# Value products, spread maxima and an earlier first score in the first attention layer

## The reference

```python
qkv = x @ w_qkv.T + b_qkv                 # 512 q, 128 k, 128 v features
q, k, v = jnp.split(qkv, [q_dim, q_dim + kv_dim], axis=-1)
q = apply_rope(q, 0)                      # 32 heads of 16
k = apply_rope(k, 0)                      # 8 heads of 16, each for 4 query heads
scores = jnp.einsum('bhqd,bhkd->bhqk', q, k) / math.sqrt(HEAD_DIM)
scores = jnp.where(causal[None, None, :, :], scores, jnp.float32(-1e+20))
attn = jax.nn.softmax(scores, axis=-1)
out = jnp.einsum('bhqk,bhkd->bhqd', attn, v)
```

## Time and profile before

| what | value |
|---|---|
| median of three runs | 1301.76 us |
| the profiled execution: device time, span | 1308.18 us, 1306.5 us |
| mean granted TensorE clock of the profiled execution | 0.925 |
| TensorE matmul busy | 1194.7 us, 91% |
| VectorE busy | 928.7 us, 71% |
| ScalarE, GpSimd busy | 656.8 us, 375.5 us |

### The profile page before, as it was taken

One profiled execution on the slowest core, in us unless ns is written; L12 is line 12 of the kernel. 1 busy time (PEld: TensorE's weight loads), 2 busy tenths in 40 slices (PEclk: granted clock), 3 DMA queues, 4 the chain that ended last, 5 costly groups with the idle time before them and its releaser, 6 DMA issues.

```text
span 1306.5 us, 21547 instructions
## 1 busy us (share of the span) xinstructions
PE 1194.7 (91%) x6800; PEld 750.8 (57%) x6800; DVE 928.7 (71%) x2974; ACT 656.8 (50%) x1007; POOL 375.5 (29%) x505
## 2 busy tenths in 40 slices
PE   4998999999899898998879999999997998989988
PEld 1875344443258787545868754444432888855478
DVE  5789898988337677653659788999881567676365
ACT  1721666666545544544436026666666464435542
POOL 0431322111144420215514313111212544002262
PEclk9997789988799999899979957999889999989999
DMA  9464412220001013200140743112200100330001
GB/s 314 135 186 82 131 28 48 60 67 2 2 1 51 1 34 90 66 2 1 65 180 9 209 112 90 30 26 59 67 3 1 51 2 1 89 99 2 1 9 57
DMA packets 40309, 80.39 MB, mean 62 GB/s; under 512 B 6060, under 2 KB 7596, under 8 KB 40060
## 3 DMA queue, kind: packets, MB, share of 16 engines
q1 hardware_dynamic: 40200, 79.02, 21.1%
HBM read 48.98 MB, written 27.08 MB: 58 GB/s over the span
## 4 chain that ended last, share of the span: by engine, by line
PE 67%; DVE 17%; POOL 5%; issue 5%; ACT 2%; DMA 2%; SPq 1%; DVEq 0%; ACTq 0%; POOLq 0%
PE bank L1012 16%; PE bank L885 12%; PE bank L792 5%; PE bank L794 5%; PE bank L793 5%; DVE maxes L1231 5%; PE bank L996 5%; DVE unused L1227 3%; PE bank L778 3%; PE bank L990 3%; PE bank L895 2%; POOL x L1517 2%; POOL w_odd L1499 2%; PE bank L817 2%; PE bank L819 2%
## 5 line engine op out<-in xcount | busy, mean ns | idle before, releaser
L1464 ACT ACTIVATE probs<-bank 128x1024 f32<-128x1024 f32 (+3 forms) x416 | 365.8, 911 | 315.7 <-PE bank L996 233.5
L885 PE MATMUL bank<-ops 48*128 48x512 f32 (+3 forms) x960 | 316.8, 434 | 14.1 <-DVE maxes L1227 4.1
L1227 DVE CUSTOM_DVE_ANT_0 unused<-bank,causal 128x128 bf16<-128x128 f32 (+3 forms) x640 | 278.5, 485 | 47.4 <-PE bank L885 43.9
L1575 POOL TENSOR_SCALAR_AFFINE_SELECT probs<-probs 128x256 f32<-128x256 f32 (+1 forms) x256 | 118.8, 464 | 605.8 <-ACT probs L1464 604.7
L885 PEld LDWEIGHTS bank<-ops 48*128 48x128 f32 (+1 forms) x960 | 161.8, 206 | 196.0 <-DVE maxes L1227 77.6
L1012 PE MATMUL bank<-probs,v_mem 128*17 128x512 f32 (+6 forms) x1920 | 253.1, 536 | 1.4 <-ACT heads_raw L1451 1.0
L1231 DVE TENSOR_REDUCE maxes<-bank 128x1 f32<-128x512 f32 x320 | 206.7, 683 | 44.0 <-PE bank L885 42.8
L996 PE MATMUL bank<-ops 50*128 50x512 f32 (+2 forms) x640 | 181.1, 463 | 3.9 <-ACT probs L1464 3.7
L792 PE MATMUL bank<-ops,xT 128*128 128x512 f32 (+1 forms) x288 | 115.5, 401 | 19.6 <-DVE x L1085 11.5
L996 PEld LDWEIGHTS bank<-ops 50*128 50x128 f32 x640 | 88.9, 204 | 61.4 <-ACT probs L1464 30.7
L1506 POOL TENSOR_TENSOR rstd<-var_eps,minus_half 128x1 f32<-128x1 f32 x96 | 52.7, 549 | 214.4 <-DVE var_eps L1063 213.8
(11 more groups left out here) (119 smaller groups left out, 1909.6 us busy)
## 6 DMA issues: line engine op xcount, KB each, us to landing
query_rows_dram<-ops SPq DMA_DIRECT2D x48, 256.0 KB, 3.8
ops<-query_rows_dram SPq DMA_DIRECT2D x64, 192.0 KB, 4.3
w_odd<-staging_wqkv SPq DMA_DIRECT2D x4, 1536.0 KB, 7.4
x<-x_dram SPq DMA_DIRECT2D x16, 256.0 KB, 6.2
ops<-features SPq DMA_DIRECT2D x64, 64.0 KB, 2.0
ops<-ops SPq DMA_DIRECT2D x16, 256.0 KB, 3.0
out_dram<-x SPq DMA_DIRECT2D x16, 256.0 KB, 2.0
staging_wqkv<-wqkv_dram SPq DMA_DIRECT2D x2, 1536.0 KB, 16.0
```

Of the source, the lines that this page charges most:

```text
L885: last = mm(dst[:, h * w:(h + 1) * w], queries(a, u)[rows, t // 4, hi, t % 4 * P:(t % 4 + 1) * P], keys(a, u, hi)[rows, HALF * kp:HALF * k ...
L1227: V.tensor_tensor_reduce(unused[:, masked % 3, 0:w], part, causal[:, HALF - w:], 1.0, NEG, ALU.add, ALU.max, dst).then_inc(s["max_done"].s ...
L1464: A.activation(probs[:, e % 6, :, 0:cols], scores[:, 2 * (e % 2):2 * (e % 2) + 2, 0:cols], ACT.Exp, scale=a.scale).then_inc(s["exp"].sem, 1)
L1575: G.affine_select(out=p, in_=p, compare_op=ALU.is_ge, fill=0.0, base=0, pattern=pattern, channel_multiplier=-1).then_inc(s["masked"].sem, 1)
```

## The change

Three things change, all in the first attention layer. A value product becomes 12 matmuls of 128 columns, each with its own weights, all into one PSUM range, and VectorE reads it with one instruction; `v_rest` is gone. `ring_in` places 16 ring items in ticks 7 to 11 instead of 12 in ticks 8 to 10, at most one behind a chunk apart from the last chunk of tick 10, which has two; four of them now stand behind the four values of tick 11. `slack` falls from 12 to 6, so the first score stands behind 22 ring items (21 maxima and the shift) instead of 28 (27 and the shift).

```diff
-            self.ring_in = {8: (0, 0, 0, 2), 9: (0, 0, 0, 5), 10: (0, 0, 0, 5)}
+            self.ring_in = {7: (0, 0, 1, 1), 8: (0, 1, 1, 1), 9: (0, 1, 1, 1), 10: (0, 1, 1, 2), 11: (1, 1, 1, 1)}
...
-A0 = Attention("rot", 32, 8, 16, 0.25, 2, True, ahead=1.07, slack=12)
+A0 = Attention("rot", 32, 8, 16, 0.25, 2, True, ahead=1.07, slack=6)
...
-                    if a.rope:
-                        both = w_odd.rearrange("p m (k n) -> p m k n", k=KC)[:, :, :, a.qk_feats:]
-                        wide = dst[:, 0:2 * n].rearrange("p (m n) -> p m n", m=2)
-                        for k in range(KC):
-                            if k < KC - 1:
-                                mm(wide, x_hi[:, k, :], both[:, :, k, :], start=(k == 0), stop=False)
-                            mm(dst[:, 0:n], x_lo[:, k, :], hi[:, k, a.qk_feats:], start=False, stop=False)
-                        last = mm(wide, x_hi[:, KC - 1, :], both[:, :, KC - 1, :], start=False, stop=True)
-                    else:
-                        for k in range(KC):
-                            mm(dst[:, 0:n], x_hi[:, k, :], hi[:, k, a.qk_feats:], start=(k == 0), stop=False)
-                            mm(dst[:, 0:n], x_hi[:, k, :], lo[:, k, a.qk_feats:], start=False, stop=False)
-                            last = mm(dst[:, 0:n], x_lo[:, k, :], hi[:, k, a.qk_feats:], start=False, stop=(k == KC - 1))
-                        between()
+                    for k in range(KC):
+                        mm(dst[:, 0:n], x_hi[:, k, :], hi[:, k, a.qk_feats:], start=(k == 0), stop=False)
+                        mm(dst[:, 0:n], x_hi[:, k, :], lo[:, k, a.qk_feats:], start=False, stop=False)
+                        last = mm(dst[:, 0:n], x_lo[:, k, :], hi[:, k, a.qk_feats:], start=False, stop=(k == KC - 1))
+                    between()
...
-                    if a.rope:
-                        V.tensor_tensor(v_rest[:, j % 2, :], src[:, n:2 * n], bias, ALU.add).then_inc(s["rest"].sem, 1)
-                        dve.wait_ge(s["rest"].sem, s["rest"].at(b, j + 1))
-                        bias = v_rest[:, j % 2, :]
```

More of the change, by code:

```diff
@@ L329, in build @@
         bias_v = {QKV0: sb("bias_v0", [P, 128]), QKV1: sb("bias_v1", [P, 256])}
-        v_rest = sb("v_rest", [P, 2, 128])
         bx = {WO0: sb("bo0", [P, D]), WO1: sb("bo1", [P, D]), MOE_A: sb("bbase", [P, D])}
@@ L487, in build @@
             s["read"] = signal(f"{n}_qkv_product_read", len(a.products))
-            s["rest"] = signal(f"{n}_v_rest", NT)
             s["turnable"] = signal(f"{n}_rope_products", 6)
```

## The result

The changed kernel takes **1318.8 us** (median of 4 executions, 1315.1 to 1324.1) against 1302.0 for the kernel before (1299.4 to 1307.0): a ratio of 1.0121, 95% interval 1.0089 to 1.0153. It is slower by 1.2%. The forecast was 1302, with 1310 as the end of its range. Six more executions of the changed kernel, taken with the last experiment, give 1.0101 (1.0047 to 1.0156).

The account below looks back on a forecast made before the run. TensorE was taken as 67% of the chain and VectorE 17%, VectorE bounding the stretch around the change. +1.2 in the first sequence and -0.7 in the second make +0.5, so 1302 from the median 1301.76; range 1294 to 1310.

Parts of the forecast that it names:

- the marker: Fixed point in the catch-up: VectorE's maximum number 21 of the first unit, 113.9 before, predicted 115.1, +1.2.
- Values: First-layer value products: twelve weight loads at 0.115 make 1.38 us each instead of 0.92, +0.46.
- Item 0's wait: Ahead of the first ring item: TensorE waits 2.1 us for the first queries, landing at 90.4.
- The clock behind that wait: Behind item 0, up to tick 11: TensorE's work from 90.4 summed at full speed, without a clock fall.
- Rival 1: Slower: TensorE's clock falls ahead of the second values in both sequences, +9.2 us, to 1311; chance 0.14.
- The matmuls of 12 items (0.1 to 0.3 each, 3.0 in all): TensorE from 90.4 to tick 11: ring item matmuls add 3.0 us, so tick 11 starts at 102.3.
- From the start of tick 11 to the shift's copy: Second values, items and shift: from 102.3 to the copy at 109.95, against 110.47 before.
- a wait of 0.9 at item 12: In tick 11, behind its first value: TensorE waits 0.9 us for the second queries, landing at 104.6.
- Copy to first score: Shift transfers on SP: 0.29 + 2.77 + 1.35 = 4.4 us, so the score can start at 114.35.
- From the score to the marker: VectorE idles for the score's 0.3 and the next item's 0.45, from 114.35 to 115.1.
- The cover: Ring items ahead of the first score no longer cover the shift transfers; VectorE idles 1.3, marker +1.2 us.
- Second sequence: Same walk: maximum number 21 at 759.2 against 759.9, -0.7 us, with TensorE holding its clock.

Follow-up runs that it names:

- Number 6: Kernel before with the changed kernel's ring item counts by tick, each tick's items in one clump, tick 11 one behind each value; ratio 1.0032.
- Experiment 5: Kernel before with ring items spread one or two behind each chunk and second value, none in tick 7; ratio 1.0028.
- the repeat: The changed kernel once more, unchanged, six more executions and a second profile; median 1314.0 us, ratio 1.0101.
- 1: Changed kernel with the ring items back at their old places, three clumps in ticks 8 to 10; ratio 1.0113.
- number 4: Kernel before with only the changed kernel's value products (12 matmuls of 128 columns) and their one VectorE read; ratio 1.0049.
- number 8: Kernel before with values in one range and one read, but 8 products of 128 columns, one low-half term left out; ratio 1.0069.
- 7: Kernel before with the last three ring items ahead of the shift spread behind values 2 to 4 of tick 11; ratio 1.0030.
- 11: Kernel before with its three clumps of ring items cut 3, 4 and 5 in place of 2, 5 and 5; ratio 1.0007.

## Why the prediction was wrong

The prediction walked from item 0 to the marker; every time is the first sequence's, aligned.

**Values: right.** 1.38 a product, 0.115 a load; the rows have 0.111. The block behind the first values starts at 77.95 (predicted 78.1). The Trainium skill, "TensorE: Matmul & The Clock Gate", section "LDWEIGHTS (loading the stationary operand)", gives columns / 1.2 in ns, for 128 columns an estimate of 107. The trace agrees (111), and the 81 ns of "Back-to-back issue gap" on the same page of the Trainium skill, which the prediction weighed, do not hold here.

**Item 0's wait: right in kind, short by 0.8.** The loads landed at 91.2, not 90.4. Their time to landing was as read (5.4 to 6.3). The sum counted it from the start of the first of the two loads, and the second starts about 0.4 later; it also left out the 0.2 by which they start later (85.58, aligned 84.42, against 84.24).

**The clock behind that wait: missing.** The sum let TensorE go on at full speed. It ran 3.4 us at half, 1.5 lost. Rival 1 tied a fall of the clock to the waits, with a chance of 0.14, but put it ahead of the second values, and there the clock was up in this trace. Of the twelve item-0 waits of 2.2 to 3.5 us in the six traces that have them, eleven are followed by such a fall within 4 us; in the other eight traces, where item 0 waits 0.6 or less, there is none at this place in sixteen passes. Number 6 has the fall in one sequence alone, and tick 11 is 1.4 later there. The same page of the Trainium skill, section "HAM oscillation — how this bites in real kernels", describes such falls in a loop that waits 3 to 5 us for a load in every pass, and prices them at half of the time at the lower level. The traces agree in kind and nearly in price (1.5 of 3.4), but ten of the twelve waits here are under 3 us, and each stands alone.

**"The matmuls of 12 items (0.1 to 0.3 each, 3.0 in all)": the step that failed most.** It counted columns streamed and no change of shape. From 92.32 to 109.11 are 16.8; 13 chunks take 8.9 and the fall 1.5, so the items took 6.4 in eleven places, 3.4 more than I had. Experiment 5 shows the same period without wait or fall. The 0.1 to 0.3 that I took is what an item of 96 rows costs in the second layer (0.23); these have 48. The Trainium skill has a rule that may bear on it and that I passed over, in "TensorEngine Tiling (Array Packing)", "Key Properties": changing the tiling mode drains TensorE. That the lost lead of the loads is such a drain would fit both layers, if 48 rows change the mode and 96 do not. No trace shows the mode, so the reason is argued; shown are the price and that the items with 96 rows do not pay it.

These three are 0.8 + 1.5 + 3.4 = 5.7, and tick 11 came at 107.95 instead of 102.3, 5.65 late. Against the kernel before, which is another comparison, the 5.5 are split otherwise: its three clumps took 102.45 - 91.55 - 8 x 0.68 = 5.4 with their waits, so the lone places cost only 1.0 more, the wait is 2.9 (from 89.41, where the chunk ahead is through, to 92.32), the fall 1.5, and 0.1 comes from ahead of item 0.

**Behind it the sum came out, in part by luck.** From the start of tick 11 to the shift's copy 7.65 were predicted and 7.54 measured. But the 7.65 hold a wait of 0.9 at item 12, which did not come because the tick was so late, and 0.25 for each of the lone items between the values, where the starts of two values with an item between them, 111.03 and 112.94, are 1.91 apart: 1.33 for the value and 0.58 for the item. The step that failed above failed here again, and the missing wait covered it. Copy to first score is right (4.4 and 4.34). From the score to the marker 1.25 passed instead of 0.75, with TensorE at its lower level since 118.0.

**The cover: under-priced.** +1.2 at the marker came from 1.7 for the cover less 0.5 for an earlier copy. There was no earlier copy (it is 5.0 and 4.0 late), and alone the cover costs 2.2 and 1.9.

**Second sequence: -0.7 predicted, +5.8 measured.** The clock did hold in tick 11, as I took it (the granted clock is 1.00 from 754 to 762), but the tick started 6.0 late by the same terms.

Both sequences give 13.0 at the marker, and 13.3 is the rest at equal lower-level time. That they agree so closely is partly luck: the set to which the trace belongs has a rest of 14.5, and in the repeat the markers are 8.6 and 6.2 late, 14.8 together, with a rest of 12.4. In its first sequence TensorE is at its lower level from 112.3, inside tick 11, where rival 1 had the fall. The other 1 to 4 us of the 14.7 to 17 between the means or medians are clock, and smaller than what single executions differ by.

**What stays open**: why the three kernels with narrow values and old places (1, 4, 8) spend about 20 us more at the lower level than the kernel before. Their profiles have part of tick 11 at half speed in the first sequence, but so have 5, 7 and 11, whose means are at 177 to 187. Until that is known, the narrow values with the old places (number 4) cost 8.8 us in the mean, of which 3.1 are explained.

## What to carry to other kernels

Price an instruction that is moved between others by what stands on both sides of it: here a ring item of 48 rows costs 0.59 us between two chunks of 128 rows and hardly more for two in one clump, and one of 96 rows costs 0.23. Price a wait of TensorE by the clock behind it too. Where a term is given a fraction of a microsecond and then counted eleven times in each of two sequences, look for a row of exactly that neighbourhood. It was there, in TensorE's timeline of the kernel before:

```profile
91.32 0.39 PE L819 MATMUL bank<-ops,w_odd 128*128 128x512 f32 x1
91.63 0.44 PE L885 MATMUL bank<-ops 48*128 48x128 f32 x4
92.01 0.50 PE L817 MATMUL bank<-ops,w_odd 128*128 128x512 f32 x1
92.35 0.39 PE L818 MATMUL bank<-ops,w_odd 128*128 128x512 f32 x1
```

Four small matmuls between two blocks take 92.35 - 91.32 = 1.03 where two steps of 0.23 would be 0.46 without them: 0.57 for two items in one clump, as much as one costs alone. And a price is to be set against what it replaces: the clumps cost 5.4 too.

## What the hardware showed beyond that

One microsecond at TensorE's lower level costs 0.30 us of this kernel's time, not 0.5; TensorE is two thirds of the chain, and half of that is 0.33. Executions of one build differ by up to 80 us in lower-level time (the kernel before: 139 to 218), so by some 20 us of span; one profile each of two builds can't tell which is faster by 1%, but with the clock beside each time ten executions tell some 2 us.

A clock fall is not certain behind a wait: with 2.28 and 2.32 us ahead of the same instructions in one execution, it came once. Nor does it need such a wait: number 8 has falls about its first values with none over 1.1 us in TensorE's timeline there.
